# A Mamba scan on one core: the B-row product placed in two PSUM banks and scanned there, with other resets of carried state and another order of the pieces

## What is computed

```python
xm, z = split(x @ W_in.T, 2)
xc = silu(causal_conv(xm, conv_w) + conv_b)          # 4 taps
dt, Bm, Cm = split(xc @ W_xproj.T, [R, R + N])       # N = 16 states
delta = softplus(dt @ W_dt.T + b_dt)
dA  = exp(delta[..., None] * A)
dBx = delta[..., None] * Bm[:, :, None, :] * xc[..., None]
h_t = dA_t * h_{t-1} + dBx_t                         # 256 channels x 16 states
y   = sum_n h_t[n] * C_t[n] + D_skip * xc;  y = y * silu(z)
out = y @ W_out.T
```

## Time and profile before

| | us |
|---|---|
| median of 3 runs | 1671.3 |
| lowest and highest | 1665.87, 1673.43 |
| the profiled execution | 1673.58 |
| its span, first instruction to last | 1671.8 |
| TensorE clock granted over the span, share of full speed | 0.829 |

### The profile page before, as it was taken

The page is one execution under the profiler, slowest core; times in us unless marked ns, Lnnn a source line. Parts: engine busy times, 40 slices in busy tenths (PEclk is TensorE's granted clock), DMA queues, the critical chain, the costliest instruction groups (busy, mean ns, idle before and its releaser), DMA issues.

```text
span 1671.8 us, 12912 instructions
## 1 busy us (share of the span) xinstructions
PE 1212.9 (73%) x3810; PEld 591.7 (35%) x3818; DVE 1173.4 (70%) x2595; ACT 606.2 (36%) x1086; POOL 395.3 (24%) x284
## 2 busy tenths in 40 slices
PE   2222784967478674967786787777979699999897
PEld 0001231333123221333322353434535355555554
DVE  6897798878978799765647789886885843443321
ACT  1510652235432543223223241513233236754443
POOL 6133042312422043221201313030320121111211
PEclk8555795979779786977888779897798899999998
DMA  5000000000000000020001000000000000000000
GB/s 181 0 0 0 1 1 0 1 0 1 0 0 0 1 0 1 1 87 1 1 0 37 20 1 1 1 1 1 1 1 1 30 27 1 7 1 7 1 7 7
DMA packets 11269, 17.74 MB, mean 11 GB/s; under 512 B 1304, under 2 KB 7584, under 8 KB 10688
## 3 DMA queue, kind: packets, MB, share of 16 engines
q1 hardware_dynamic: 11200, 16.93, 2.9%
HBM read 15.88 MB, written 1.05 MB: 10 GB/s over the span
## 4 chain that ended last, share of the span: by engine, by line
PE 31%; DVE 16%; ACT 4%; issue 2%; POOL 1%; POOLq 0%; DVEq 0%; ACTq 0%
PE bankE L1663 7%; PE bankE L1741 5%; PE bankE L1132 3%; DVE b_yt L1458 2%; PE bankS L1705 1%; DVE b_m L1417 1%; PE bankE L518 1%; PE bankS L1183 1%; DVE b_pT L1430 1%; DVE c_tw L1833 1%; PE bankE L544 1%; DVE b_pT L1240 1%; DVE b_xnS L1240 1%; PE bankS L1182 1%; PE bankS L1690 1%
## 5 line engine op out<-in xcount | busy, mean ns | idle before, releaser
L284 POOL TENSOR_TENSOR cv<-cv,hc 128x1024 f32<-128x1024 f32 x60 | 141.4, 2356 | 308.0 <-DVE hc L683 307.7
L676 DVE TENSOR_TENSOR_SCAN hs<-dA,carry,dbx 128x512 f32<-128x512 f32 x128 | 185.6, 1490 | 3.9 <-ACT dA L358 0.5
L1663 PE MATMUL bankE<-c_h,c_w 128*128 128x512 f32 x288 | 152.3, 611 | 9.5 <-DVE c_tw L1833 6.6
L1636 ACT ACTIVATE c_h<-bankE,C 128x512 f32<-128x512 f32 x144 | 98.8, 688 | 120.8 <-PE bankE L1741 120.5
L395 ACT ACTIVATE sg<-bankE,C 128x512 f32<-128x512 f32 x80 | 54.9, 687 | 176.7 <-PE bankE L518 176.7
L1833 DVE SCALAR_TENSOR_TENSOR c_tw<-bankE,C,wb_ready 128x512 f32<-128x512 f32 x32 | 24.0, 750 | 131.4 <-PE bankE L1663 131.4
L449 PE MATMUL bankS<-bc,sel 96*128 96x512 bf16 x64 | 31.0, 484 | 102.1 <-DVE hc L683 89.0
L1741 PE MATMUL bankE<-c_fH,c_w1H 128*128 128x512 f32 x144 | 101.4, 704 | 0.0
L358 ACT ACTIVATE dA<-dl,Aneg 128x512 f32<-128x512 f32 x128 | 81.1, 709 | 26.6 <-DVE hs L676 26.5
L488 PE MATMUL bankE<-h2T,wg 128*128 128x512 f32 x128 | 74.8, 668 | 18.8 <-ACT sg L380 18.8
L1532 POOL TENSOR_TENSOR c_acc<-c_acc,c_tw 128x512 f32<-128x512 f32 x32 | 40.7, 1271 | 191.0 <-DVE c_tw L1833 190.8
(11 more groups left out here) (478 smaller groups left out, 2714.5 us busy)
## 6 DMA issues: line engine op xcount, KB each, us to landing
c_w<-in_w SPq DMA_DIRECT2D x1, 2304.0 KB, 8.7
X<-in_x SPq DMA_DIRECT2D x4, 256.0 KB, 4.2
wg<-in_gate_T SPq DMA_DIRECT2D x1, 1024.0 KB, 7.4
wu<-in_up_T SPq DMA_DIRECT2D x1, 1024.0 KB, 9.4
f<-in_w SPq DMA_DIRECT2D x1, 1024.0 KB, 6.7
out<-X SPq DMA_DIRECT2D x4, 256.0 KB, 2.3
b_wq<-in_Wqkv SPq DMA_DIRECT2D x1, 768.0 KB, 4.4
g<-in_sw SPq DMA_DIRECT2D x2, 256.0 KB, 3.4
```

What stands on the lines that cost most here:

```text
L284: pool.tensor_tensor(cv[:, :, :], cv[:, :, :], hc[:, k % 2, :, :], ALU.add).then_inc(s["y_acc"], 1)
L676: V.tensor_tensor_scan(hs[:, h, :], dA[:, (HV * k + h) % DA, :], dbx[:, h, :], carry[:, k, h:h + 1], ALU.mult, ALU.add).then_inc(s["scan_d ...
L1636: act.activation(h[:, n % 3, :], E[k % 2][:, :], ACT.Gelu_apprx_tanh, bias=col("b1_3", k)).then_inc(s["c_h"], 1)
L1663: pe.matmul(E[2][:, :], w2[:, k, :], h[:, n % 3, :], start=(f == 0), stop=(f == FB3 - 1)).then_inc(s["c_down"], 1)
```

## The change

`dbx` is no longer a tile in SBUF. The four S banks are allocated as one PSUM tensor, and `dbx` is its banks 1 and 2. B_k is spread into bank 2, C_k into bank 0. So the DVE product at `Nk` reads bank 2 and writes bank 1 (head 0) and bank 2 (head 1, in place), and the two recurrences read their second input from PSUM. They run head 1 first, which frees bank 2; PE spreads B_{k+1} when that first recurrence is done, in piece `ok` instead of `nk`. `dA` tiles are made in the same new order of heads. The banks for the `delta` projection are renamed to suit.

The columns `keep` and `fresh` leave the constants. Where a group ends a sequence, `carry`, the tail of `xm`, and in lane b the first columns are set by a memset; elsewhere they are copied by a `tensor_tensor` with both inputs the same and the operation max. A group that ends a sequence makes no `carry` copies at all (groups 1 and 3), and one that doesn't has nothing at the head of `B1` (groups 0 and 2).

`ORDER` is a new table. It holds the same pieces; many stand elsewhere.

```diff
-    dbx = sb("dbx", [P, HV, G])
+    dbx = bank[:, 1:3, :]
+    LATER_FIRST = (1, 0)
...
-                    n, h = divmod(t, HV)
+                    n, h = t // HV, LATER_FIRST[t % HV]
...
-                pe.matmul(S[1][:, :], sel[:, NS + k, :], bc3[:, :], start=True, stop=True).then_inc(s["Cb_ready"], 1)
-            elif p[0] == "n" and k + 1 < NS:
-                at_least(pe, s["dbx_done"], i, NS, k + 1)
-                pe.matmul(S[0][:, :], sel[:, k + 1, :], bc3[:, :], start=True, stop=True).then_inc(s["Bb_ready"], 1)
+                pe.matmul(S[0][:, :], sel[:, NS + k, :], bc3[:, :], start=True, stop=True).then_inc(s["Cb_ready"], 1)
+            elif p[0] == "o" and k + 1 < NS:
+                at_least(pe, s["scan_done"], i, HV * NS, HV * k + 1)
+                pe.matmul(S[2][:, :], sel[:, k + 1, :], bc3[:, :], start=True, stop=True).then_inc(s["Bb_ready"], 1)
...
-                V.tensor_scalar(xm[:, :, 0:KC - 1], xm[:, :, G:G + KC - 1], col_at("keep", i), None, ALU.mult).then_inc(s["tail_kept"], 1)
+                tail = xm[:, :, G:G + KC - 1]
+                ins = V.memset(xm[:, :, 0:KC - 1], 0.0) if ends_batch(i) else V.tensor_tensor(xm[:, :, 0:KC - 1], tail, tail, ALU.max)
+                ins.then_inc(s["tail_kept"], 1)
...
-                V.tensor_tensor(dbx[:, :, :], dx[:, :, :], S[0][:, :].unsqueeze(1).to_broadcast([P, HV, G]), ALU.mult).then_inc(s["dbx_done"], 1)
+                V.tensor_tensor(dbx[:, :, :], dx[:, :, :], S[2][:, :].unsqueeze(1).to_broadcast([P, HV, G]), ALU.mult).then_inc(s["dbx_done"], 1)
...
-                for h in range(HV):
-                    at_least(V, s["dA_ready"], i, HV * NS, HV * k + h + 1)
-                    if h == 0:
+                for q, h in enumerate(LATER_FIRST):
+                    at_least(V, s["dA_ready"], i, HV * NS, HV * k + q + 1)
+                    if q == 0:
                         at_least(V, s["dbx_done"], i, NS, k + 1)
-                    V.tensor_tensor_scan(hs[:, h, :], dA[:, (HV * k + h) % DA, :], dbx[:, h, :], carry[:, k, h:h + 1],
+                    V.tensor_tensor_scan(hs[:, h, :], dA[:, (HV * k + q) % DA, :], dbx[:, h, :], carry[:, k, h:h + 1],
                                          ALU.mult, ALU.add).then_inc(s["scan_done"], 1)
...
-                inc(V.tensor_copy(carry[:, k, :], hs[:, :, G - 1]))
+                if not ends_batch(i):
+                    inc(V.tensor_tensor(carry[:, k, :], hs[:, :, G - 1], hs[:, :, G - 1], ALU.max))
             elif p == "B1":
-                wait()
-                inc(V.tensor_scalar(carry[:, :, :], carry[:, :, :], col_at("keep", i), None, ALU.mult))
+                if ends_batch(i):
+                    wait()
+                    inc(V.memset(carry[:, :, :], 0.0))
...
+        def first_column(t, g, fresh):
+
+            if ends_batch(g):
+                return dve.memset(t[:, 0:1], fresh)
+            return dve.tensor_tensor(t[:, 0:1], t[:, G:G + 1], t[:, G:G + 1], ALU.max)
...
-        S = [ctx.enter_context(nc.psum_tensor(f"bankS{i}", [P, G], F32)) for i in range(4)]
+        bank = ctx.enter_context(nc.psum_tensor("bankS", [P, 4, G], F32))
+        S = [bank[:, i, :] for i in range(4)]
```

More of the change, by code:

```diff
@@ L436, in piece @@
                 for h in range(HV):
[L437 removed]
+                    pe.matmul(S[h][:, :], wdt[:, h * P:(h + 1) * P], dtT[:, :], start=True, stop=True).then_inc(s["dpre_ready"], 1)
             elif p == "F4":
@@ L441, in piece @@
                 at_least(pe, s["bc_split"], i, 1, 1)
-                pe.matmul(S[0][:, :], sel[:, 0, :], bc3[:, :], start=True, stop=True).then_inc(s["Bb_ready"], 1)
+                pe.matmul(S[2][:, :], sel[:, 0, :], bc3[:, :], start=True, stop=True).then_inc(s["Bb_ready"], 1)
             elif p[0] == "N":
@@ L2019, in sandwich @@
         experts = Region(nc, MAMBA_END, SBUF[1])
-        lanes = {"a": mamba_and_experts(*shared, mamba, experts)}
+        lanes = {"a": mamba_and_experts(*shared, mamba, experts, bank)}
         assert mamba.at <= MAMBA_END, mamba.at
```

113 lines of the change are left out of this document (54 added, 59 removed).

## The result

| us | before | after |
|---|---|---|
| median | 1671.4 (4 runs, 1665.9 to 1673.4) | 1625.5 (4 runs, 1619.4 to 1633.3) |
| ratio of the times | | 0.973, 95% interval 0.968 to 0.978 |
| span of the profiled execution | 1671.8 | 1631.5 |
| granted TensorE clock over the span | 0.829 | 0.841 |

The change gains 46 us in the median and 40.3 us between the two profiled executions; the profiled one of the changed kernel is the slowest of its four. The forecast was 1646 with a range of 1631 to 1661: the sign and the mechanism in the recurrences were right, the forecast gain was too small by 20 us, and the term that failed is the one for the new order.

What follows compares the result with a forecast made beforehand. Up to 718 us DVE's queue sets the time, wholly in group 0, mostly in later groups. Terms 12.9 + 9.4 - 2 + 1.5 + 3 = 24.8 us off the median 1671.3 give 1646; range 1631 to 1661, 8 in 10.

Steps and rivals of the forecast that it cites:

- part 4: New order of pieces: waits ahead of the first `dbx` shrink, 1 us a group, 3 us gained.
- the weight splits: Lane c's splits on POOL, earlier and four in a row: taken as 0, with 5 us either way in the range.
- part 1: Recurrences no longer stretched by POOL's adds: 12.9 us gained in group 0, 9.4 of 15.6 in groups 1 to 3.
- part 2: PSUM operands of 128 recurrences and 64 products on DVE: 2 us lost, 11.7 as the other bound.
- Rival D: Product reading and writing bank 2 in one pass takes double for that half: 34 us more, 1680; chance 0.05.
- part 3: Copies and resets: 32 copies into `carry` vanish, 1.5 us gained, 2.2 at most; removing `B1`'s multiplication worth nothing.
- A: Groups 1 to 3 give nothing because PE and ACT are late by DVE's gain: 12 us left, 1659; chance 0.12.
- B: All the stretching, copies and order gained, no PSUM cost: 40 us, 1631; chance 0.11.
- C: Recurrences still stretched, through their other SBUF reads: only 2 or 3 us gained, 1669; chance 0.06.
- E: `dbx` waits 0.5 us for the next B row in 48 states beside experts: 24 us go, 1670; chance 0.04.
- F: New two-SBUF-input copies wait for POOL's add: 32 copies, 75 us less the 5 they take, 1716; chance 0.02.

Runs made afterwards that it cites:

- the control: The changed kernel run once more with nothing altered: 1625.2 us, ratio 0.972 against the kernel before.
- the front moves alone: Changed kernel with the old order, except M2, M3, M4 placed as in the new order in the fronts of groups 1 to 3: 1662.9 us, ratio 0.996.
- PSUM alone: Changed kernel with the old order and the old resets and copies: 1662.2 us, ratio 0.996 against the kernel before.

## Why the prediction was wrong, point by point

**The order (part 4) is the term that failed.** I took 3 us, 1 a group, with 9 as the bound, and called 0 for everything else that the table moves. It measures 13.6 us in the fronts and 8.2 in the last experts' stage, 21.8 with the recurrences reading PSUM: 18.8 us more than I took. By the profiled executions the whole sum is 15.5 us short (40.3 against 24.8), so my other terms together come out 3.3 us below what I gave them. Three faults are in the term.

- The waits of the earlier trace rows I read rightly and priced at a third. "The work isn't gone, only the waiting can be": in group 1 the waiting did go in full, 3.07 us, and in group 3 too. Group 2 still has two products there, and 1.99 us of its 2.68 stay. From `dx` to the first `dbx` the three groups take 3.85, 0.78 and 3.63 us less. The product and its wait in the states cost nothing visible (139.3 us with the old order, 139.1 with the new, in group 1), where DVE is idle for 20.6 us. The run with M1 behind F9 brought exactly these waits back.
- I looked only right ahead of the first `dbx`. The front has a second place, before `dl`: there the product of M2 and its `tw` were on DVE's and PE's path. The timelines of before and of after, DVE in group 1's front:

```profile
184.69 0.68 DVE L636 CAST bc<-bankS 32x512 bf16<-32x512 f32 x1
...
188.99 0.69 DVE L733 TENSOR_TENSOR hh<-sg,bankE 128x512 f32<-128x512 f32 x1 [0.56 <-ACT sg L380]
189.79 0.69 DVE L838 TENSOR_TENSOR tw<-bankE,wb 128x512 f32<-128x512 f32 x1
...
191.56 1.61 DVE L648 TENSOR_SCALAR dl<-bankS,C 128x512 f32<-128x512 f32 x2 [1.08 <-ACT dA L346]
```
```profile
171.76 0.68 DVE L643 CAST bc<-bankS 32x512 bf16<-32x512 f32 x1
...
176.78 1.61 DVE L655 TENSOR_SCALAR dl<-bankS,C 128x512 f32<-128x512 f32 x2 [1.28 <-ACT dA L351]
```

  From the cast to the first `dl` it is 6.87 us before and 5.02 after, and the same 1.85 us in groups 2 and 3: 5.5 of the 13.6.
- I took everything from 718 us on at the same length, and watched only for time gained or lost after lane a. 8.2 us fell before that, in lane a's last stage, beside lane b's first group. Behind it my 0 held: lane b and the end are 2.8 us longer in the first profile and 0.3 in the control, so the weight splits, which I gave 5 us either way, cost nothing that can be told.

**The terms don't add, which no rival of mine said.** The fronts can be emptied only if the states can take the pieces. Without PSUM they can't: 19 us come back there, 5.4 of them because more adds meet more recurrences. With the front moves alone they can't either, since the pieces pile up in the first state. So order and PSUM form have to be priced together. The old order with PSUM gains some 10 us (8.7 with the old resets), the new order without it loses 3 to 4 (with the new resets it gains 2 to 3), both together gain 46.

**The stretching (part 1) was right.** Group 0 gives 12.9 us as forecast, to 0.1. The three later groups' states give 8.3 us where 9.4 (and a part of the copies' 1.5) stood, with more expert products in them. That the waiting comes back was right too: in "PSUM alone" 7.8 of the 15.6 us appear, a half where I took 0.6. The Trainium skill (SBUF — State Buffer, Who interferes with whom) says that a DVE instruction with two SBUF inputs contends with a GpSimd instruction that reads SBUF, and one with at most one SBUF input doesn't. The 3.82 us pair beside a 2.18 us add, and 2.45 beside 1.27 with `dbx` in PSUM, agree.

**PSUM operands (part 2) cost nothing that can be told.** I took 2 us lost, with 11.7 as the bound. The product writes PSUM at 1222 ns against 1214: 64 times 8 ns, 0.5 us. A recurrence that no add stretches has a median of 1260 ns with its second input in either place, and a pair takes 2.45 us in both the earlier trace rows. So there is neither the loss nor a gain, as I had excluded; the fall of the whole line's median from 1277 is the stretching. The extra 62 cycles that the Trainium skill (VectorE: DVE Perf Modes, The TRN2 errata) gives for a PSUM source, 8.3 us by my estimate, don't show in the recurrence, the one operation whose source moved. Rival D, the in-place write, is out by the product's 1222 ns.

**Copies and resets (part 3) were about right**: 1.5 forecast, 3 measured with an interval of 1 to 5. The add was the multiplication's cover and stayed: DVE now waits for it openly, by the table of waits over the 16 states of group 1 in the changed kernel.

```profile
DVE cv L701 <- POOL cv L289: 2.4, 1, 2.4
```

**The rivals.** A (the later groups give nothing) and C (still stretched) are out. B, all of it and the order, came nearest, with 1631, and I gave it 0.11; even its 9 us for the order were too few. E doesn't occur, but is real: it is what the order of the heads avoids. F is out.

## What to carry to other kernels

When two DVE inputs lie in SBUF beside GpSimd adds, moving one into PSUM frees both engines; what that is worth is set by how many of these meetings fall where DVE sets the pace, so it must be priced together with any change that moves work there. When a table moves pieces out of a crowded stage, look at every place in the stage where the moved piece stood between two steps of the chain, and at the state in which they land: left side by side there they are paid back in full (5.7 us off the front of group 1, 6.9 on its states). When a matmul waits for another engine, price the queue behind it on PE and not only the wait of its reader.

## What was not expected of the hardware

- One order of lane b's pieces took 418 or 427 us in different kernels, 5.6 us of it in a single run of 112 matmuls at a mean granted clock of 1.00 or 0.80, and the kernel that was traced twice at 427.1 repeated it to 0.1 us. An edit worth 22 us ahead of it lost 9 there.
- The recurrence costs the same with its second input in PSUM as in SBUF: a median of 1260 ns where no add stretches it.
- Four matmuls of the front took 3.43 us at a granted clock of 0.56 behind 3.48 us of idle PE, and 1.95 at 1.00 with an expert's matmuls ahead of them.
- The `acc` add of POOL is held up by the recurrences as these are by it: 2.18 us instead of 1.27.
